# Projections, expert keys and the first output product on column tiles of 32, and the last exponents' turn exchanged with the first projection

## The chip, the cores and the metric

One core of one Trainium2 chip runs the whole kernel. The metric is device time in microseconds (us) of one execution; the kernel before takes 973.56 us, the median of 3 runs (973.54 to 974.25).

## The reference, cut to what matters

The input x has 128 batches, 64 features and 750 time steps. Everything is float32. In short:

```
h = token pooling of x            # windows of 8, softmax of a score over the window: [128, 94, 64]
n = layernorm(h)
q, k = n @ Q_h, n @ K_h           # 8 heads of rank 32, folded into one matrix per head: scores = n (K_h^T Q_h) n^T / 8
h = h + sum_h softmax(scores_h) @ n @ VO_h
n = layernorm(h)
sx = n @ hl_w                     # 4 heads of 16
q (4 experts), k, v of sx; causal softmax per head and expert; gate over the experts
h = h + two small layers, layernorm and a gate over the heads of that mixture
```

## The kernel before

The 128 batches are worked in 32 quads of 4 batches. A quad's data has 4 x 96 = 384 token columns (94 used). The instructions of every engine are written out by hand in a fixed order. One pass of `quad` holds parts of several quads at once: the token pooling of quads g+1 to g+3, the attention of quad g, the mix and the output product of quad g-1, the expert keys of quad g-2, and the expert attention of quad g-3. All stages exist for g = 3 to 31, which is 29 passes; those before fill the pipeline and those after drain it. Engines are ordered by semaphores only.

TensorE's order around the change is as follows (names of functions, then lines):

- `turn_p3(1, 5)` and `turn_p3(3, 4)` (L784), each four transposes of 128x96 shifted scores of the experts; ScalarE then takes their exponents out of PSUM with `exp_p3`.
- waits, among them for `s_shifted2` (VectorE's last subtraction, L1452) and for `r1_hx` (ScalarE has read bank 7).
- `project(.., 0, 0, 1)` (L687): the attention's first projection, two matmuls with 64 rows (rows 0 to 63 and 64 to 127 of the array) and 128 columns of weights, moving 384 columns, to banks 0 and 1. It sets `at_pa`.
- `turn_p3(6, 7)`: the last four transposes of the experts' scores, 128x128, to bank 7.
- `front_pair(1, 2, 3)` (L733): two matmuls of the same 64x128 form, to banks 2 and 3. It sets `f_kb`.
- waits for `exp_p3(3, 4)` (bank 4 is free) and for the first `copy_k` of the quad (`at_q`, bank 1 is free).
- `front_last(4, 1)`: one 64x128 matmul on rows 0 to 63 (L733) and, on rows 64 to 127, four matmuls with 96 columns of weights that move 64 columns each (L744). It sets `f_kc`.
- `pool_x` (L639, 128x32), `front_pair(0, 3, 7)` (L733, sets `f_ka`), `project(.., 1, 1, 6)` (sets `at_pb`), `mix` (L705, 32x64), `score` 0 (L695, 64x32 on 8 tiles, 376 columns).
- later `score` 1, `give_outT` (L713: eight matmuls with 128 rows and 64 columns, 192 moving columns), in every second quad `tok_score` (L625, L632), then `score` 2.

`turn_c` (L813, 128x32) multiplies, for each expert, four column tiles of mixed values with one moving operand of 84 columns.

ScalarE's order in the same stretch: `exp_p3(1)`, `exp_p3(3)`, `copy_k(1)` (waits for `at_pa`, reads bank 1, sets `at_q`), `exp_p3(6)`, two `front_kp` (wait for `f_kb`), `front_vc` (waits for `f_kc`, reads bank 1), one `front_kp`, `copy_k(0)`, `store_h`, `front_sxT` (waits for `f_ka`), `front_kp`, two `copy_k` (wait for `at_pb`).

In the trace each float32 matmul stands as two MATMUL records, each with its own LDWEIGHTS record. Below, one such record is called a pass. "64x128" means 64 rows and 128 columns of weights.

Of the kernel before, what the change touches and what calls it, by code (L numbers as in the profile page):

```python
# [15 lines left out]
TP = 96  # L16
HEADS, RANK = 8, 32
NH, NE, HD = 4, 4, 16
QB = 32
# [11 lines left out]
def exists(m, total):  # L31

    return not isinstance(m, int) or 0 <= m < total
# [10 lines left out]
def audio_tower(nc, x, tok_w, tok_b, attn_q, attn_k, attn_vo, hl_w, hl_b, wq, wk, wv, gate_w, gate_b,  # L44
                ln_g, ln_b, fc1_w, fc1_b, fc2_w, fc2_b, fnorm_g, fnorm_b, fgate_w, out):
    with ExitStack() as ctx:
        def sb(name, shape, dt=F32):
            return ctx.enter_context(nc.sbuf_tensor(name, shape, dt))

        def sem(name):  # L50
            return ctx.enter_context(nc.semaphore(name))


        psum = ctx.enter_context(nc.psum_tensor("psum", [128, 8, 512], F32))
# [9 lines left out]
        g_w = sb("g_w", [128, 2, 128])  # L64
        vo_w = sb("vo_w", [128, HEADS // 2, NFEAT])
# [68 lines left out]
        xT = sb("xT", [128, 2, 4, TP])  # L134
# [6 lines left out]
        cT = sb("cT", [128, HP, NT, 4, TB])  # L141
        oT = sb("oT", [128, NT, 2, TB])
        aq = sb("aq", [128, NE, NH, 32])
        wsx = sb("wsx", [128, NH, 32])
        wtok = sb("wtok", [128, 2, NH, HD])
# [24 lines left out]
        x3T = sb("x3T", [128, 4, TP])  # L170
# [89 lines left out]
        f_ka = sem("f_ka")  # L260
        f_kb = sem("f_kb")
# [9 lines left out]
        p_turned = sem("p_turned")  # L271
# [336 lines left out]
        def _(pe):  # L608
# [73 lines left out]
                mm.then_inc(at_turned, 1)  # L682

            def project(p, i, low, high):
                for half in range(2):
                    rows = slice(64 * half, 64 * half + 64)
                    mm = pe.matmul(psum[:, (low, high)[half], 0:4 * TP], g_w[rows, i, :], xT[rows, p, :, :].rearrange("p b t -> p (b t)"),  # L687
                                   start=True, stop=True)
                mm.then_inc(at_pa if i == 0 else at_pb, 1)

            def score(p, j, low, high):
# [17 lines left out]
            def give_outT(bank):  # L709

                for hp in range(HP):
                    for half in range(2):
                        mm = pe.matmul(psum[64 * half:64 * half + 64, bank, 0:NT * 64].rearrange("p (j c) -> p j c", j=NT), vo_w[:, hp, :],  # L713
                                       cT[:, hp, :, 2 * half:2 * half + 2, :].rearrange("p j b t -> p j (b t)"),
                                       start=(hp == 0), stop=(hp == HP - 1))
                mm.then_inc(at_outT, 1)

            def give_out(bank):
# [9 lines left out]
                    mm = pe.transpose(psum[:, bank, 128 * j:128 * j + 128], xn3[:, j, :, :].rearrange("p a f -> p (a f)"), ident)  # L728
                mm.then_inc(f_turned, 1)

            def front_k(half, w, bank):
                rows = slice(64 * half, 64 * half + 64)
                return pe.matmul(psum[:, bank, 0:NJ * 128], w[rows], x3T[rows, :, :].rearrange("p b t -> p (b t)"), start=True, stop=True)  # L733

            def front_pair(k, low, high):

                front_k(0, wsx[:, :, :].rearrange("p n d -> p (n d)") if k == 0 else aq[:, 1, :, :].rearrange("p n d -> p (n d)"), low)
                front_k(1, aq[:, 0 if k == 0 else 2, :, :].rearrange("p n d -> p (n d)"), high).then_inc(f_ka if k == 0 else f_kb, 1)

            def front_last(low, high):  # L740

                front_k(0, aq[:, 3, :, :].rearrange("p n d -> p (n d)"), low)
                for b in range(4):
                    mm = pe.matmul(psum[0:TP, high, 64 * b:64 * b + 64], x3T[64:128, b, :],  # L744
                                   wtok[64:128, 0, :, :].rearrange("k n d -> k (n d)"), start=True, stop=True)
                mm.then_inc(f_kc, 1)

            def front_resid(bank):
# [25 lines left out]
            def turn_p3(f, bank):  # L774
                j = ORDER[PT_J[f]]
                for e in range(NE):
                    if j == 2:
                        src, rows = pu3[2][:, e, f, :], TP
                    elif j == 1:
                        n, a = 2 * (f - 4) + e // 2, e % 2  # L780
                        src, rows = pu3[1][:, n, 2 * a:2 * a + 2, :].rearrange("p e u -> p (e u)"), 128
                    else:
                        src, rows = pu3[0][:, e, :, :].rearrange("p n u -> p (n u)"), 128
                    mm = pe.transpose(psum[0:rows, bank, 128 * e:128 * e + 128], src, ident)  # L784
                mm.then_inc(p_turned, 1)
# [43 lines left out]
            def quad(q):  # L829
                for v in range(4):  # L830
                    g = 4 * q + v
# [61 lines left out]
                            pe.wait_ge(x_scaled, 3 * g + 5)  # L893
                    if exists(g - 2, NQUAD):
                        pe.wait_ge(f_xT, g - 1)
                    if exists(g, NQUAD):
                        project(v % 2, 0, 0, 1)
                    if exists(g - 3, NQUAD):
                        turn_p3(6, 7)
                    if g + 1 == 0:  # L900
                        pe.wait_ge(tok_ready, ((g + 1) // 2) + 1)
                        make_g(0)
                    if exists(g - 2, NQUAD):
                        front_pair(1, 2, 3)
                        if exists(g - 3, NQUAD):
                            pe.wait_ge(p_copied, 7 * g - 17)
                        else:
                            pe.wait_ge(at_xT, g + 1)
                        if exists(g, NQUAD):
                            pe.wait_ge(at_q, 4 * g + 1)  # L910
                        else:
                            pe.wait_ge(s_shifted2, 2 * g - 4)
                    if exists(g + 1, NQUAD):
                        pe.wait_ge(x_scaled, 3 * g + 6)
                    if exists(g - 2, NQUAD):
                        front_last(4, 1)
# [9 lines left out]
                    if exists(g - 2, NQUAD):  # L926
                        front_pair(0, 3, 7)
                    if exists(g, NQUAD):
                        project(v % 2, 1, 1, 6)
# [158 lines left out]
            for q in range(-1, 12):  # L1088
                quad(q)

        @block.scalar
        def _(act):
# [34 lines left out]
            def copy_k(p, hp, bank):  # L1127
                act.activation(kp[:, p, :, hp, :], psum[:, bank, 0:4 * TP].rearrange("p (b t) -> p b t", b=4),  # L1128
                               ACT.Copy).then_inc(at_q, 1)
# [43 lines left out]
            def exp_p3(f, bank):  # L1173

                i = PT_J[f]
                j = ORDER[i]
                rows = TP if j == 2 else 128
                act.activation(pT3[j][:, f - (0, 4, 6)[i], :, :, :].rearrange("p e b t -> p (e b t)"), psum[0:rows, bank, :], ACT.Exp).then_inc(  # L1178
                    p_copied, 1)
# [21 lines left out]
            def quad(q):  # L1201
                for v in range(4):
                    g = 4 * q + v
# [55 lines left out]
                    if exists(g - 2, NQUAD):  # L1259
                        act.wait_ge(p_turned, 7 * g - 11)  # L1260
                        exp_p3(1, 5)
                        act.wait_ge(p_turned, 7 * g - 10)
                        exp_p3(3, 4)
                    if exists(g + 1, NQUAD):
                        act.wait_ge(at_pa, g + 2)
                        copy_k((v + 1) % 2, 1, 1)
                    if exists(g - 2, NQUAD):
                        act.wait_ge(p_turned, 7 * g - 9)
                        exp_p3(6, 7)
                    if exists(g - 1, NQUAD):  # L1270
                        act.wait_ge(f_kb, g)
                        front_kp((v + 1) % 2, 2, 3)
# [51 lines left out]
            for q in range(-1, 12):  # L1324
                quad(q)
# [398 lines left out]
```

## Time and profile before

| | |
|---|---|
| median of 3 runs | 973.56 us |
| the profiled execution's own time | 976.96 us |
| its span | 975.2 us |
| PE busy | 896.4 us (92%) |
| DVE, ACT, POOL busy | 815.2, 730.6, 718.2 us |

PE is TensorE's matmuls, PEld its weight loads, DVE is VectorE, ACT ScalarE, POOL GpSimd. Busy time of PE holds the modelled end of each matmul, so neighbouring groups overlap by some tenths of a microsecond; the starts are recorded. A row of windows gives the stretch, its length, the busy time (instructions) of PE, PEld, DVE, ACT and POOL, the granted TensorE clock (1.00 is 2.4 GHz), the DMA share and GB/s. Lines are those of the kernel before.

### The profile page before, as it was taken

The numbers are of one execution on the slowest core, as the hardware profiler recorded it, in microseconds if no ns is written. First come the engines' busy times: TensorE is split into PE (matmuls) and PEld (weight loads), VectorE is DVE, ScalarE is ACT, GpSimd is POOL, SyncE is SP. The second block draws the span as 40 slices with busy tenths as digits, with TensorE's granted clock in tenths as the row PEclk, the third lists the DMA queues.
The fourth block names the chain that finished last, engine by engine and source line by source line (L and its number), as shares of the span: only waits on it lengthen the run. The fifth ranks groups of instructions, "written<-read, shape, count | busy, mean of one in ns | idle before, by whom it ended". The sixth has DMA issues, their size and how long they took to land.

```text
span 975.2 us, 44187 instructions
## 1 busy us (share of the span) xinstructions
PE 896.4 (92%) x18600; PEld 572.2 (59%) x18600; DVE 815.2 (84%) x1917; ACT 730.6 (75%) x2759; POOL 718.2 (74%) x1052
## 2 busy tenths in 40 slices
PE   4788999999999999999999999999999999989841
PEld 4355656666666666666666666666666666556530
DVE  4455887889898988889898988989898998889877
ACT  1676788888878888888878888888778888885520
POOL 3233345677888887878888887878889888879893
PEclk9787999999999999999999999999999999999975
DMA  6310111110111101111111111111100000000001
GB/s 202 105 40 8 36 42 43 41 42 11 46 46 46 42 12 43 46 46 46 46 46 46 27 30 39 44 47 46 46 15 14 7 14 13 14 13 16 18 8 17
DMA packets 41157, 36.77 MB, mean 38 GB/s; under 512 B 27520, under 2 KB 30720, under 8 KB 40960
## 3 DMA queue, kind: packets, MB, share of 16 engines
q1 hardware_dynamic: 40406, 33.91, 12.4%
q8 instruction: 147, 2.41, 1.0%
q14 instruction: 50, 0.41, 0.1%
q10 hardware_dynamic: 554, 0.05, 0.0%
HBM read 25.08 MB, written 3.08 MB: 29 GB/s over the span
## 4 chain that ended last, share of the span: by engine, by line
PE 71%; ACT 16%; DVE 9%; POOL 2%; issue 1%; DMA 1%; POOLq 0%; ACTq 0%; DVEq 0%
ACT pu L1135 14%; PE psum L784 10%; PE psum L705 7%; PE psum L733 6%; PE psum L813 6%; PE psum L687 5%; PE psum L695 5%; PE psum L769 4%; PE psum L614 4%; PE psum L639 3%; PE psum L713 3%; PE psum L803 2%; PE psum L826 2%; PE psum L799 2%; DVE pu L1452 2%; PE psum L822 2%
## 5 line engine op out<-in xcount | busy, mean ns | idle before, releaser
L1135 ACT ACTIVATE pu<-psum,mx 128x94 f32<-128x94 f32 x768 | 247.4, 370 | 8.3 <-DVE mx L1420 6.9
L1135 ACT ACTIVATION_READ_ACCUMULATOR pu<-psum,mx 128x1 f32 x768 | 182.2, 238 | 0.0
L1420 DVE TENSOR_REDUCE mx<-psum 128x8 f32<-128x752 f32 x96 | 90.1, 940 | 88.0 <-PE psum L695 83.9
L478 POOL TENSOR_TENSOR pu<-pu,pr 128x752 f32<-128x752 f32 x96 | 138.7, 1447 | 28.0 <-DVE pr L1424 27.7
L1178 ACT ACTIVATE pT<-psum 96x512 f32<-96x512 f32 (+1 forms) x224 | 131.3, 601 | 36.3 <-PE psum L784 32.8
L512 POOL TENSOR_TENSOR st<-st,neg_half 128x12 f32<-128x12 f32 x64 | 146.0, 2281 | 5.0
L784 PE MATMUL psum<-ident_w,pu 128*96 128x128 f32 (+1 forms) x896 | 136.4, 283 | 13.1 <-ACT pu L1135 7.3
L1449 DVE TENSOR_REDUCE mx<-psum 128x16 f32<-128x1536 f32 (+2 forms) x96 | 116.4, 1213 | 10.3 <-PE psum L769 10.1
L784 PEld LDWEIGHTS psum<-ident_w,pu 128*96 128x96 f32 (+1 forms) x896 | 97.0, 134 | 47.4 <-issue 17.2
L1452 DVE TENSOR_TENSOR pu<-psum,mx 128x1536 f32<-128x1536 f32 (+2 forms) x96 | 117.6, 1225 | 3.3
L695 PE MATMUL psum<-kp,xT 64*32 64x376 f32 x1536 | 83.4, 491 | 8.3 <-ACT pu L1135 6.2
L1428 DVE STREAM_TRANSPOSE pT<-pu 128x768 f32<-128x768 f32 x96 | 87.7, 941 | 0.0
L733 PE MATMUL psum<-x3T,aq 64*128 64x384 f32 x256 | 79.6, 528 | 0.0
L1140 ACT ACTIVATE cT<-psum 128x384 f32<-128x384 f32 x128 | 53.9, 494 | 33.6 <-PE psum L705 33.5
L813 PE MATMUL psum<-gx,ct 128*32 128x84 f32 x3072 | 77.8, 240 | 0.9 <-issue 0.9
L813 PEld LDWEIGHTS psum<-gx,ct 128*32 128x32 f32 x3072 | 58.3, 110 | 25.5 <-issue 24.8
L1182 ACT ACTIVATE oc<-psum 128x336 f32<-128x336 f32 x96 | 43.1, 448 | 39.7 <-PE psum L813 39.5
L705 PE MATMUL psum<-pT,xn 32*64 32x384 f32 x1536 | 70.1, 489 | 0.3 <-ACT kp L1163 0.3
L1128 ACT ACTIVATE kp<-psum 128x384 f32<-128x384 f32 x128 | 59.9, 501 | 13.3 <-PE psum L687 13.3
L769 PE MATMUL psum<-kp,sxT 32*32 32x256 f32 (+2 forms) x3072 | 69.3, 390 | 0.0
L1460 DVE SCALAR_TENSOR_TENSOR ct<-sxT,psum 128x512 f32<-128x512 f32 x96 | 65.5, 682 | 3.7 <-PE psum L803 1.5
L529 POOL TENSOR_TENSOR ft<-ft,fx 128x192 f32<-128x192 f32 x29 | 17.2, 593 | 69.2 <-DVE ft L1528 69.2
(179 smaller groups left out, 2189.1 us busy)
## 6 DMA issues: line engine op xcount, KB each, us to landing
xs<-in_x SPq DMA_DIRECT2D x64, 375.0 KB, 3.9
vb<-va SPq DMA_DIRECT2D x32, 128.0 KB, 2.2
out_h<-ho SPq DMA_DIRECT2D x126, 16.0 KB, 1.4
out_h<-ho SPq DMA_DIRECT2D x126, 7.5 KB, 1.4
vc<-va SPq DMA_DIRECT2D x96, 16.0 KB, 2.3
gx<-in_L_ffn_gate_w SPq DMA_DIRECT2D x16, 0.2 KB
fc<-in_L_ffn_fc_w SPq DMA_DIRECT2D x12, 1.0 KB
fc<-in_L_ffn_fc_b SPq DMA_DIRECT2D x12, 0.1 KB
```

The lines of the kernel that those rows point to most:

```text
L478: pool.tensor_tensor(p, p, bcast(pr[:, j, :, :].rearrange("p a b -> p (a b)"), 2, NTOK), ALU.mult).then_inc(at_normed, 1)
L512: pool.tensor_tensor(st[:, k, 3, :], st[:, k, 2, :], neg_half[:, 0:NJ * NH], ALU.pow).then_inc(rstd, 1)
L695: mm = pe.matmul(psum[TB * b:TB * b + TB, (low, high)[par], 0:HP * NTOK], xT[rows, p, b, TB * j:TB * j + TB], kp[rows, p, b, :, 0:NTOK], s ...
L705: mm = pe.matmul(psum[64 * par:64 * par + 64, banks[b], 0:HP * TP], xn[rows, r, ub, 0, :], pT[rows, :, par, :, ub, :], start=(ub == 0), st ...
L733: return pe.matmul(psum[:, bank, 0:NJ * 128], w[rows], x3T[rows, :, :].rearrange("p b t -> p (b t)"), start=True, stop=True)
L769: mm = pe.matmul(psum[QB * b:QB * b + QB, bank + n, 0:NE * w].rearrange("p (e u) -> p e u", e=NE), sxT[rows, p, j, QB * b:QB * b + QB], kp ...
L784: mm = pe.transpose(psum[0:rows, bank, 128 * e:128 * e + 128], src, ident)
L813: mm = pe.matmul(psum[rows, bank, GC * e:GC * e + GC], mixed[:, rows], gx[:, e, :], start=True, stop=True)
L1135: ins = act.activation(pu[:, j, par, hp, 0:NTOK], psum[:, (low, high)[par], NTOK * hp:NTOK * hp + NTOK], ACT.Exp, bias=mx[:, j, par, hp:hp ...
L1178: act.activation(pT3[j][:, f - (0, 4, 6)[i], :, :, :].rearrange("p e b t -> p (e b t)"), psum[0:rows, bank, :], ACT.Exp).then_inc(p_copied, 1)
L1449: dve.tensor_reduce(mx3[:, i, :, :], S3(j, bank), AX.X, ALU.max).then_inc(shifted, 1)
L1452: dve.tensor_tensor(p, S3(j, bank), bcast(mx3[:, i, :, :], 3, QB * (j + 1)), ALU.subtract).then_inc(shifted, 1)
```

## The change

`project`, `front_pair` and `front_last` split their 64x128 matmuls into four of 64x32, each to its own 32 partitions of PSUM, and the 64x96 token matmuls into three of 64x32. `give_outT` splits each 128x64 matmul into two of 128x32. The moving columns of each matmul stay as they were. On TensorE `turn_p3(6, 7)` is moved ahead of the first projection, and on ScalarE `exp_p3(6, 7)` ahead of `copy_k(1)`.

```
             def project(p, i, low, high):
-                for half in range(2):
-                    rows = slice(64 * half, 64 * half + 64)
-                    mm = pe.matmul(psum[:, (low, high)[half], 0:4 * TP], g_w[rows, i, :], xT[rows, p, :, :]...
+                for c in range(4):
+                    for half in range(2):
+                        rows = slice(64 * half, 64 * half + 64)
+                        mm = pe.matmul(psum[32 * c:32 * c + 32, (low, high)[half], 0:4 * TP], g_w[rows, i, 32 * c:32 * c + 32], ...
...
             give_outT:
-                        mm = pe.matmul(psum[64 * half:64 * half + 64, bank, ...], vo_w[:, hp, :], cT[...], ...
+                        for c in range(2):
+                            q = 64 * half + 32 * c
+                            mm = pe.matmul(psum[q:q + 32, bank, ...], vo_w[:, hp, 32 * c:32 * c + 32], cT[...], ...
...
             def front_pair(k, low, high):
-                front_k(0, wsx[...] if k == 0 else aq[:, 1, ...], low)
-                front_k(1, aq[:, 0 if k == 0 else 2, ...], high).then_inc(f_ka if k == 0 else f_kb, 1)
+                for n in range(NH):
+                    front_k(0, n, wsx[:, :, :] if k == 0 else aq[:, 1, :, :], low)
+                    mm = front_k(1, n, aq[:, 0 if k == 0 else 2, :, :], high)
+                mm.then_inc(f_ka if k == 0 else f_kb, 1)
 
             def front_last(low, high):
-                front_k(0, aq[:, 3, ...], low)
+                for n in range(NH):
+                    front_k(0, n, aq[:, 3, :, :], low)
                 for b in range(4):
-                    mm = pe.matmul(psum[0:TP, high, 64 * b:64 * b + 64], x3T[64:128, b, :], wtok[...])
+                    for j in range(NJ):
+                        mm = pe.matmul(psum[QB * j:QB * j + QB, high, 64 * b:64 * b + 64], x3T[64:128, b, QB * j:QB * j + QB], wtok[...])
...
             TensorE's order:
+                    if exists(g - 3, NQUAD):
+                        turn_p3(6, 7)
                     if exists(g, NQUAD):
                         project(v % 2, 0, 0, 1)
-                    if exists(g - 3, NQUAD):
-                        turn_p3(6, 7)
...
             ScalarE's order:
+                    if exists(g - 2, NQUAD):
+                        act.wait_ge(p_turned, 7 * g - 9)
+                        exp_p3(6, 7)
                     if exists(g + 1, NQUAD):
                         act.wait_ge(at_pa, g + 2)
                         copy_k((v + 1) % 2, 1, 1)
-                    if exists(g - 2, NQUAD):
-                        act.wait_ge(p_turned, 7 * g - 9)
-                        exp_p3(6, 7)
```

## Rows read from the trace of the kernel before

**Rows 1.** Page, part 1: busy time of each engine.

```profile
PE 896.4 (92%) x18600; PEld 572.2 (59%) x18600; DVE 815.2 (84%) x1917; ACT 730.6 (75%) x2759; POOL 718.2 (74%) x1052
```

**Rows 2.** Windows of two neighbouring quads, the second with `tok_score`.

```profile
500.76:527.80 27.04, 26.39 (x555) 16.69 (x554) 24.59 (x59) 22.56 (x87) 23.18 (x35) 1.00 0.14 41
527.80:555.60 27.80, 27.75 (x602) 17.86 (x602) 24.55 (x59) 22.76 (x87) 22.45 (x33) 1.00 0.14 41
```

**Rows 3.** Waits of TensorE in the same two quads: total, times, longest.

```profile
PE psum L784 <- ACT pu L1135: 0.4, 1, 0.4
PE psum L695 <- ACT pu L1135: 0.2, 1, 0.2
```

**Rows 4.** Timeline of TensorE, from `turn_p3(1)` to `score` 0: start, length, passes.

```profile
499.79 1.04 PE L784 MATMUL psum<-ident_w,pu 128*96 128x128 f32 x8
500.76 0.92 PE L687 MATMUL psum<-xT,g_w 64*128 64x384 f32 x4
501.61 0.66 PE L784 MATMUL psum<-ident_w,pu 128*128 128x128 f32 x4
502.19 1.23 PE L733 MATMUL psum<-x3T,aq 64*128 64x384 f32 x5
502.95 0.56 PE L744 MATMUL psum<-wtok,x3T 64*96 64x64 f32 x5
...
503.35 0.41 PE L744 MATMUL psum<-wtok,x3T 64*96 64x64 f32 x3
503.69 0.86 PE L639 MATMUL psum<-xt,pick 128*32 128x192 f32 x16
504.48 0.59 PE L733 MATMUL psum<-x3T,wsx 64*128 64x384 f32 x1
...
505.23 0.81 PE L687 MATMUL psum<-xT,g_w 64*128 64x384 f32 x4
505.97 2.19 PE L705 MATMUL psum<-pT,xn 32*64 32x384 f32 x48
508.09 0.86 PE L695 MATMUL psum<-kp,xT 64*32 64x376 f32 x16
508.88 0.69 PE L826 MATMUL psum<-fc,hxm 128*128 128x96 f32 x4
```

**Rows 5.** Single lines in this quad: ns min/median/max, first and last start.

```profile
L687 PE MATMUL psum<-xT,g_w x8: 482/482/587, 500.8 to 505.6; 64*128 64x384 f32 x8
L695 PE MATMUL psum<-kp,xT x48: 474/475/500, 508.1 to 513.6; 64*32 64x376 f32 x48
L713 PE MATMUL psum<-cT,vo_w x16: 326/326/377, 511.4 to 512.6; 128*64 128x192 f32 x16
```

**Rows 6.** Timeline of TensorE's weight loads in `score` 0.

```profile
508.09 0.18 PEld L695 LDWEIGHTS psum<-kp,xT 64*32 64x32 f32 x16 [0.60 <-issue]
```

**Rows 7.** Timeline of TensorE before the next quad: `turn_c`, then transposes in a row.

```profile
522.34 0.80 PE L813 MATMUL psum<-gx,ct 128*32 128x84 f32 x32
...
526.39 0.60 PE L614 MATMUL psum<-ident_w,xs 128*128 128x128 f32 x4
526.83 1.04 PE L784 MATMUL psum<-ident_w,pu 128*96 128x128 f32 x8
```

**Rows 8.** Timeline of ScalarE in the stretch of rows 4.

```profile
500.43 1.08 ACT L1178 ACTIVATE pT<-psum 96x512 f32<-96x512 f32 x2 [0.49 <-PE psum L784]
501.72 0.49 ACT L1128 ACTIVATE kp<-psum 128x384 f32<-128x384 f32 x1 [0.21 <-PE psum L687]
502.30 0.60 ACT L1178 ACTIVATE pT<-psum 128x512 f32<-128x512 f32 x1
503.16 0.87 ACT L1163 ACTIVATE kp<-psum 128x384 f32<-128x384 f32 x2 [0.26 <-PE psum L733]
```

**Rows 9.** Timeline of VectorE: its last subtraction before this stretch, and its wait after it.

```profile
499.86 0.69 DVE L1452 TENSOR_TENSOR pu<-psum,mx 128x512 f32<-128x512 f32 x1
...
509.06 0.94 DVE L1420 TENSOR_REDUCE mx<-psum 128x8 f32<-128x752 f32 x1 [1.55 <-PE psum L695]
```

More of the change, by code:

```diff
@@ L684, in project @@
             def project(p, i, low, high):
-                for half in range(2):
-                    rows = slice(64 * half, 64 * half + 64)
-                    mm = pe.matmul(psum[:, (low, high)[half], 0:4 * TP], g_w[rows, i, :], xT[rows, p, :, :].rearrange("p b t -> p (b t)"),
-                                   start=True, stop=True)
+                for c in range(4):
+                    for half in range(2):
+                        rows = slice(64 * half, 64 * half + 64)
+                        mm = pe.matmul(psum[32 * c:32 * c + 32, (low, high)[half], 0:4 * TP], g_w[rows, i, 32 * c:32 * c + 32],
+                                       xT[rows, p, :, :].rearrange("p b t -> p (b t)"), start=True, stop=True)
                 mm.then_inc(at_pa if i == 0 else at_pb, 1)
@@ L712, in give_outT @@
                     for half in range(2):
-                        mm = pe.matmul(psum[64 * half:64 * half + 64, bank, 0:NT * 64].rearrange("p (j c) -> p j c", j=NT), vo_w[:, hp, :],
-                                       cT[:, hp, :, 2 * half:2 * half + 2, :].rearrange("p j b t -> p j (b t)"),
-                                       start=(hp == 0), stop=(hp == HP - 1))
+                        for c in range(2):
+                            q = 64 * half + 32 * c
+                            mm = pe.matmul(psum[q:q + 32, bank, 0:NT * 64].rearrange("p (j c) -> p j c", j=NT), vo_w[:, hp, 32 * c:32 * c + 32],
+                                           cT[:, hp, :, 2 * half:2 * half + 2, :].rearrange("p j b t -> p j (b t)"),
+                                           start=(hp == 0), stop=(hp == HP - 1))
                 mm.then_inc(at_outT, 1)
@@ L729, in front_turn, with front_k @@
                 mm.then_inc(f_turned, 1)
-            def front_k(half, w, bank):
+            def front_k(half, n, w, bank):
                 rows = slice(64 * half, 64 * half + 64)
-                return pe.matmul(psum[:, bank, 0:NJ * 128], w[rows], x3T[rows, :, :].rearrange("p b t -> p (b t)"), start=True, stop=True)
+                return pe.matmul(psum[32 * n:32 * n + 32, bank, 0:NJ * 128], w[rows, n, :], x3T[rows, :, :].rearrange("p b t -> p (b t)"),
+                                 start=True, stop=True)
             def front_pair(k, low, high):
-                front_k(0, wsx[:, :, :].rearrange("p n d -> p (n d)") if k == 0 else aq[:, 1, :, :].rearrange("p n d -> p (n d)"), low)
-                front_k(1, aq[:, 0 if k == 0 else 2, :, :].rearrange("p n d -> p (n d)"), high).then_inc(f_ka if k == 0 else f_kb, 1)
+                for n in range(NH):
+                    front_k(0, n, wsx[:, :, :] if k == 0 else aq[:, 1, :, :], low)
+                    mm = front_k(1, n, aq[:, 0 if k == 0 else 2, :, :], high)
+                mm.then_inc(f_ka if k == 0 else f_kb, 1)
             def front_last(low, high):
-                front_k(0, aq[:, 3, :, :].rearrange("p n d -> p (n d)"), low)
+                for n in range(NH):
+                    front_k(0, n, aq[:, 3, :, :], low)
                 for b in range(4):
-                    mm = pe.matmul(psum[0:TP, high, 64 * b:64 * b + 64], x3T[64:128, b, :],
-                                   wtok[64:128, 0, :, :].rearrange("k n d -> k (n d)"), start=True, stop=True)
+                    for j in range(NJ):
+                        mm = pe.matmul(psum[QB * j:QB * j + QB, high, 64 * b:64 * b + 64], x3T[64:128, b, QB * j:QB * j + QB],
+                                       wtok[64:128, 0, :, :].rearrange("k n d -> k (n d)"), start=True, stop=True)
                 mm.then_inc(f_kc, 1)
```

## The prediction

> **What bounds the kernel now.** I read the page's busy times first: TensorE is busy 92% of the span with VectorE next at 84% [rows 1]. An average can't say who ends last, so I took the windows of single quads. The middle of the run is a pair of quads of 27.04 and 27.80 us. In both TensorE is busy nearly all the time, 26.39 and 27.75 us; VectorE has 24.6 us of work, ScalarE 22.7, GpSimd 23, and the granted clock is 1.00, 2.4 GHz [rows 2]. Then the waits: in the two quads TensorE waits 0.4 us before the last transposes and 0.2 us before `score` 2, both times for ScalarE's exponents of the attention [rows 3]. So the quad has two parts. From `score` 0 to the end of these exponents ScalarE decides in every second quad, and TensorE has slack. From there through the next `score` 0 TensorE decides alone. The moved and re-tiled work lies in the second part, but for `give_outT`. VectorE waits 1.55 us for `score` 0 [rows 9], so it isn't what holds that part back. What is taken off TensorE there should shorten the quad; what is taken off between `score` 0 and `score` 2 is worth something only in the quads with `tok_score`, where TensorE doesn't wait.
>
> **What a block of matmuls costs.** The starts in rows 4 split a block into three pieces. A pass of 384 columns streams for 0.32 us: `front_pair(0)` and `project` 1 have the same form and follow each other, and each is two such passes on both row halves at once. A change of form costs a drain: `project` 1 has no change before it and one after, and takes 505.97 - 505.23 = 0.74 us, so the drain is 0.10 less the 0.01 by which its second tile starts later, about 0.09 us. The first weight load after the drain isn't hidden: the first pass is 587 ns long where the later ones are 482, so a load of 128 columns adds 0.105 us; with 64 columns it is 377 - 326 = 0.05, with 32 columns 500 - 475 = 0.025 us [rows 5]. `project` 0, with a change on both sides, then is 0.105 + 0.64 + 0.01 + 0.09 = 0.85, and the row says 501.61 - 500.76 = 0.85. `score` on eight 64x32 tiles is 508.88 - 508.09 = 0.79 for 376 columns: 0.627 of streaming, 0.025 of load, 0.09 of drain, and 0.05 by which the eighth tile starts after the first (some 6.5 ns each) [rows 4]. All eight stream together. That four column tiles may also read the same moving columns is shown by L813, whose four tiles share one moving operand: its 32 passes of 84 columns are over in 0.80 us [rows 7], and one at a time they would take 32 x 0.07 = 2.2.
>
> **The change on TensorE, in the quad of rows 4.** I lay the new order out on that clock.
>
> - The eight passes of `turn_p3(1)` and `(3)` start at 499.79. They take 8 x 0.109 = 0.87 (four transposes with no change of form take 526.83 - 526.39 = 0.44 [rows 7]). `turn_p3(6)` is of their form, so it follows at 500.66 with neither drain nor exposed load, and takes 0.44 where it took 502.19 - 501.61 = 0.58. Its wait is for VectorE's subtraction, done at 499.86 + 0.69 = 500.55 [rows 9], 0.11 before, and that is enough for a release of about 0.05. If it were late it would cost what it is late.
> - Drain, 0.09: `project` 0 starts at 501.19, 0.43 later than now. Its first pass takes 0.32 + 0.025, its second starts at 501.54 (the eighth tile at 501.58).
> - `front_pair(1)` now has the form of the block before it and starts at 501.86, without drain or load; it needs 0.64 and would be over at 502.50.
> - `front_last` waits for bank 1, which `copy_k(1)` must have read. `project` 0 ends at 501.58 + 0.48 = 502.06 (now 500.76 + 0.92 = 501.68). ScalarE starts 0.04 after the end and takes 0.49 [rows 8]: 502.59. With a release of some 0.06 the matmuls start at 502.66. That is a new stall of 0.16 us in a place that has none now. ScalarE itself is in time: its two exponents start 0.48 apart from 500.43, so `exp_p3(6)`, turned by 501.26, goes from 501.39 to 501.99, in front of the copy.
> - `front_last` from 502.66: four 64x32 tiles on rows 0 to 63 take 0.345 + 0.32 + 0.02 of stagger, then 0.09 of drain: 0.78, against 503.69 - 502.95 = 0.74 now. The tokens beside it are three tiles of eight short passes. Now they follow each other at 0.08 us: the eighth ends at 503.76 and lasts at most 0.25, so it starts at 503.51, (503.51 - 502.95) / 7. With 32 columns to load instead of 96 I take at most that, and at least the 0.053 that 64 columns stream; eight of them end with the keys or before. So `pool_x` starts at 503.44, 0.25 before its 503.69.
> - `pool_x` is unchanged, 0.79: 504.23. `front_pair(0)` takes 0.665 there, where it took 0.75, and `project` 1 takes 0.64 + 0.05 + 0.09 = 0.78 against 0.74. `mix` starts at 505.67, now 505.97.
>
> The sum is 0.30 us a quad in front of `mix`. By its terms: up to `front_last` one drain is left of three (0.18), and of first loads of 0.105, 0.05 and 0.105 one of 0.025 (0.235), with rounding and stagger 0.45 (503.0 - 502.5); `front_pair(0)` gives 0.085; against that stand 0.16 of stall, 0.04 in `front_last` and 0.04 of stagger in `project` 1.
>
> **What waits behind it.** ScalarE's copies for `f_kb` start at 501.86 + 0.32 + 0.05 + 0.48 = 502.71 where they start at 503.16 now [rows 8], and the later ones follow TensorE's 0.25 to 0.3 earlier. VectorE's 1.55 us before `score` 0 becomes 1.25. From `score` 0 on everything is shifted as one. The two waits of rows 3 stay as they are, since exponents and matmuls between them start from the same `score` 0. No DMA is moved, and no queue but those of TensorE and ScalarE.
>
> **`give_outT`.** Each tile still streams eight passes of 192 columns. The first load is 0.05 less 0.025, the stagger of two more tiles takes 0.013 back: 0.01 us. In the quads without `tok_score` it goes into the wait before `score` 2.
>
> **More instructions.** 86 more passes and as many loads a quad, to 555 or 602 now [rows 2]. In `score` 0 sixteen loads, with eight passes among them, are issued in 0.18 us [rows 6], 0.011 a load. A set of eight new passes needs 0.09 us of issue under 0.32 of streaming, so I cost it at nothing. If none of it were hidden it would be 86 x 0.011 = 0.95 us a quad, but `score` itself would then be longer than its row.
>
> One rule of the Trainium skill speaks against all this ("TensorE: Matmul & The Clock Gate", The mechanism): a weight load overlaps with running matmuls only if its row group differs. The column tiles of one block share their row groups, so by that rule each of the ten steps from one set of passes to the next would show its load, and the time would be that of the third rival. The trace says no: the sixteen loads of `score` 0 are all issued by 508.27, while its first passes run until 508.59, in the same row groups [rows 5, 6].
>
> **The sum.** 29 quads (g = 3 to 31) times 0.30 us is 8.7 us; `give_outT` adds 0.01 x 15 = 0.15, and the filling and draining quads, which have the projections or the keys but not both, about 0.3. Together 9.1 us. The profiled execution took 976.96 us by its own time (975.2 of span), 3.4 above the median; 9.1 less is 967.9 there and 964.5 against the median of 973.56.
>
> **Rivals.**
>
> - *No stall.* `front_last` doesn't have to wait, because `project`'s passes or the copy end earlier than modelled. Matmul ends are modelled in the trace, which speaks for it; that ScalarE now starts 0.04 after the modelled end speaks against. The gain is 0.46 x 29 = 13.4 us: 960.1. Chance 0.10.
> - *A wait takes half.* The pull of 0.3 us makes something else late: the subtraction before the moved transposes (0.11 in hand), or the bank of `front_last` (each 0.1 us more of ScalarE costs 0.1). At 0.15 a quad, 4.4 us remain: 969.2. For it: VectorE is busy 24.6 of 27.4 us [rows 2]. Against: it waits 1.55 once a quad. Chance 0.13.
> - *Loads show after all.* Ten steps x 0.025 us = 0.25 a quad, leaving 0.05: 1.5 us, 972.1. Against it rows 6, and `mix`, with six steps in 2.12 us where streaming is 1.92 [rows 4]. Chance 0.03.
> - *The tokens queue behind the keys.* In `front_last` the token passes are issued behind eight passes of keys instead of two. If they can't overtake the second set of keys, they start 0.36 late, and the block lasts 0.36 + 7 x 0.08 + 0.18 = 1.10 instead of 0.78 us. That takes the whole 0.30 and leaves 974.0. Against it: now the first token starts beside the key's first pass, 0.32 before its second [rows 4]. For it: only one waiting pass is overtaken there. Chance 0.04.
> - *Slower: the tokens go one at a time.* There are 24 token passes instead of 8, all on rows 64 to 127, short, and beside running keys. If their three column tiles don't overlap, they need 24 x 0.053 = 1.27 us, and with the 0.13 behind them `front_last` lasts 1.40 instead of 0.78. That costs 0.62, more than the 0.30: 0.32 x 29 = 9.3 us slower, 982.9. It decides from 0.04 us a pass on, where the block is 0.30 longer. Against it: L813, whose four tiles overlap at much the same size [rows 7]. For it: no block now mixes long and short passes on several column tiles. Chance 0.07.
>
> **How the numbers follow.** The forecast has 0.61. A measurement of this kernel can tell about 0.2%, 1.9 us, from no change. Faster: forecast, no stall and half, 0.84. Same: the two rivals that leave next to nothing, 0.07. Slower: the tokens one at a time, and 0.02 for something I don't see, 0.09. The range goes from 960.0, where the stall is gone, to 971.0, past the half gain, and leaves out the other cases.
>
> **What would show it.** After the change a quad pair should last 54.84 - 0.61 = 54.23 us; `turn_p3(6)` should follow at 0.109 a pass; `front_pair(1)` should start 0.67 after `project` 0; a wait of 0.16 for ScalarE's `kp` (L1128's copy) should stand before `front_last`; `mix` should start 5.88 after `turn_p3(1)`, now 6.18. I am wrong if the tile blocks last over 0.80 us, if the tokens reach past the keys, or if the waits for L1135 grow by what the front gave.

## The result: no faster, and 0.16% slower

The changed kernel takes 976.18 us (median of 22 runs, 973.21 to 978.31), the kernel before on the same chip 974.19 (22 runs, 973.12 to 975.73): ratio 1.0016, 95% interval 1.0009 to 1.0023. The forecast was 964.5. The profiled execution of after took 974.74 us (span 973.0); it lies 1.4 under its median, where that of before lay 2.8 above the 974.19. They differ in their first slices of granted clock, so their 2.2 us of difference are not a gain: I compare stretches at clock 1.00.

The page of after: busy times, part 2's clock in the run-in, the instruction queue of part 3, and the chain by engine.

```profile
PE 888.9 (91%) x21352; PEld 552.6 (57%) x21352; DVE 817.7 (84%) x1917; ACT 730.3 (75%) x2759; POOL 717.4 (74%) x1052
...
PEclk9897999999999999999999999999999999999975
...
q8 instruction: 169, 2.77, 1.2%
...
PE 72%; ACT 16%; DVE 7%; issue 2%; POOL 2%; DMA 1%; POOLq 0%; ACTq 0%; DVEq 0%
```

The same lines of before, whose busy times are in [rows 1]; the forecast did not use them:

```profile
PEclk9787999999999999999999999999999999999975
...
q8 instruction: 147, 2.41, 1.0%
...
PE 71%; ACT 16%; DVE 9%; POOL 2%; issue 1%; DMA 1%; POOLq 0%; ACTq 0%; DVEq 0%
```

2,752 more passes and as many loads, 22 more packets in the instruction queue, and "issue" is 2% of the chain where it was 1%. ("Issue" is time in which the engine waited for nothing that the profile shows. 42,704 TensorE instructions over 169 packets are 253 each, 37,200 over 147 also 253: a packet of 16 KB, 2.77 MB over 169, holds some 250 of them.)

The windows of after: the two neighbouring quads that answer to [rows 2], from `mix` to `mix`, then twenty quads at once.

```profile
505.28:532.23 26.95, 26.23 (x648) 16.11 (x640) 24.58 (x59) 22.56 (x88) 23.15 (x34) 1.00 0.15 43
532.23:559.93 27.70, 27.55 (x694) 17.41 (x686) 24.70 (x59) 22.78 (x88) 22.44 (x34) 1.00 0.14 40
...
202.61:752.02 549.41, 539.36 (x13258) 335.77 (x13251) 492.84 (x1154) 452.58 (x1721) 454.92 (x658) 1.00 0.14 39
```

The same twenty quads of before:

```profile
203.68:753.21 549.53, 541.99 (x11533) 345.72 (x11531) 490.86 (x1155) 452.98 (x1720) 455.27 (x658) 1.00 0.14 38
```

So there are two misses. An undisturbed pair of quads is 54.65 us where it was 54.84: 0.19 gained, not 0.61. And twenty quads don't keep even that: ten undisturbed pairs would be 546.5, and 549.41 passed, 2.9 more; before it was 548.4 and 549.53, 1.1 more.

TensorE's timeline in one quad of after, which answers to [rows 4]:

```profile
499.30 1.38 PE L790 MATMUL psum<-ident_w,pu 128*96 128x128 f32 x11
500.60 0.88 PE L688 MATMUL psum<-xT,g_w 64*32 64x384 f32 x16
501.27 1.43 PE L736 MATMUL psum<-x3T,aq 64*32 64x384 f32 x20
502.20 0.48 PE L750 MATMUL psum<-wtok,x3T 64*32 64x64 f32 x15
...
502.95 0.94 PE L639 MATMUL psum<-xt,pick 128*32 128x192 f32 x16
503.83 0.51 PE L736 MATMUL psum<-x3T,wsx 64*32 64x384 f32 x1
...
504.50 0.85 PE L688 MATMUL psum<-xT,g_w 64*32 64x384 f32 x16
505.28 2.19 PE L706 MATMUL psum<-pT,xn 32*64 32x384 f32 x48
507.40 0.86 PE L696 MATMUL psum<-kp,xT 64*32 64x376 f32 x16
```

ScalarE in the same stretch, as in [rows 8]:

```profile
499.82 1.57 ACT L1184 ACTIVATE pT<-psum 96x512 f32<-96x512 f32 x3 [0.49 <-PE psum L790]
501.58 0.49 ACT L1134 ACTIVATE kp<-psum 128x384 f32<-128x384 f32 x1 [0.19 <-PE psum L688]
502.23 0.87 ACT L1169 ACTIVATE kp<-psum 128x384 f32<-128x384 f32 x2 [0.15 <-PE psum L736]
```

Set from `project` 0 on, the forecast and these rows say: `front_pair(1)` at 0.67 and 0.67; first token of `front_last` at 1.5 and 1.60; `pool_x` at 2.25 and 2.35; `front_pair(0)` at 3.04 and 3.23; `project` 1 at 3.71 and 3.90; `mix` at 4.48 and 4.68. From the first transpose of `turn_p3(1)`, at 499.19, to `mix` it is 6.09 us; the forecast was 5.88, before it was 6.18. Every block on small tiles has the length that I gave it. What is missing stands in two places: 0.10 ahead of `front_last`, and 0.09 in `pool_x`, which now lasts 0.88 instead of 0.79 [rows 4]. The twelve transposes of `turn_p3` and `project` 0, at 500.60, are 1.41 apart: 12 x 0.109 and one drain.

What the quads lose on top is in other blocks. Two timelines of TensorE in after: `turn_c` where it is undisturbed, and one quad earlier where it isn't.

```profile
494.58 0.80 PE L819 MATMUL psum<-gx,ct 128*32 128x84 f32 x32
495.32 0.64 PE L790 MATMUL psum<-ident_w,pu 128*96 128x128 f32 x4
```

```profile
466.55 0.50 PE L819 MATMUL psum<-gx,ct 128*32 128x84 f32 x15
467.25 0.55 PE L819 MATMUL psum<-gx,ct 128*32 128x84 f32 x17 [0.20 <-issue]
467.73 0.64 PE L790 MATMUL psum<-ident_w,pu 128*96 128x128 f32 x4
```

From `turn_c` to `turn_p3` it is 0.74 us in the first and 1.18 in the second, in the middle of a block, and the profile shows nothing that the engine waited for. The DMA view of 464 to 469 us, in 40 slices of 0.125:

```profile
DMA  0000050000000000000000000000000000060000
...
q8 instruction: 2, 0.03, 2.9%
```

The only transfers are two packets of instructions, one begun at about 464.7, the next at 468.4. The late pass, at 467.25, comes 2.5 us after the first began. Between 91 and 860 us `turn_c` has 3 passes in before that stopped the block for over 0.1 us, 10 in after and 11 each in `e2` and `e4` (experiments below), and all 35 came 2.2 to 2.8 us behind the start of a packet; if they fell anywhere, some 13% of them would lie in that stretch (0.7 of 5.2 us, an estimate). In `mix` and `score` of `e2` it was 1.5 to 3.9.

In this trace two packets never begin less than 3.3 us apart, at the shortest 3.2 to 3.5 in the other kernels, though their mean distance is 5.2 here, 6.0 in before and 5.2 to 6.5 in the others. That isn't for want of demand. In an undisturbed stretch of after (a `mix3`, a `score3` and part of a `turn_c` lie in it) TensorE's 124 passes and 127 loads take 2.54 us:

```profile
519.46:522.00 2.54, 2.54 (x124) 1.80 (x127) 2.36 (x5) 1.86 (x5) 2.54 (x5) 1.00 0.04 10
```

Some 250 instructions per 3.3 us is 13 ns each, and in this stretch they go at 10. In a dense block sixteen loads and eight passes are issued in 0.18 us, 8 ns each [rows 6].

### The profile page after: what moved, and what is told of

Same layout as the page of the kernel before. It is cut to its first block, busy times and chain, and to the rows that moved or that the text cites. A ratio compares the mean times of both kernels' runs of the same rounds, so it can differ in the third digit from the quotient of the medians.

```text
span 973.0 us, 49691 instructions
## 1 busy us (share of the span) xinstructions
PE 888.9 (91%) x21352; PEld 552.6 (57%) x21352; DVE 817.7 (84%) x1917; ACT 730.3 (75%) x2759; POOL 717.4 (74%) x1052
## 3 DMA queue, kind: packets, MB, share of 16 engines
q8 instruction: 169, 2.77, 1.2%
## 4 chain that ended last, share of the span: by engine, by line
PE 72%; ACT 16%; DVE 7%; issue 2%; POOL 2%; DMA 1%; POOLq 0%; ACTq 0%; DVEq 0%
ACT pu L1141 14%; PE psum L790 10%; PE psum L706 7%; PE psum L819 7%; PE psum L736 6%; PE psum L696 5%; PE psum L688 5%; PE psum L775 5%; PE psum L614 4%; PE psum L639 3%; PE psum L716 3%; PE psum L809 2%; PE psum L832 2%; PE psum L805 2%; PE psum L828 2%
## 5 line engine op out<-in xcount | busy, mean ns | idle before, releaser
L1184 ACT ACTIVATE pT<-psum 96x512 f32<-96x512 f32 (+1 forms) x224 | 128.3, 600 | 33.8 <-PE psum L790 32.5
L790 PE MATMUL psum<-ident_w,pu 128*96 128x128 f32 (+1 forms) x896 | 129.9, 280 | 13.7 <-ACT pu L1141 7.2
L736 PE MATMUL psum<-x3T,aq 64*32 64x384 f32 x1024 | 82.3, 493 | 1.6
```

What stands on the lines that cost most here:

```text
L736: return pe.matmul(psum[32 * n:32 * n + 32, bank, 0:NJ * 128], w[rows, n, :], x3T[rows, :, :].rearrange("p b t -> p (b t)"), start=True, s ...
```

## The experiments

My theory after the result: the block model holds, the 0.10 is the wait for bank 1, and the rest is TensorE's supply of instructions. The rivals: the exchange or the tiles don't do what they say; the time is lost behind `score` 0. Each time below is a median, with the ratio to the kernel before on the same chip (its medians in the four rounds of experiments were 974.64, 974.42, 973.54 and 974.91). Kernels of different rounds are compared by their ratios. "Undisturbed pair" is the sum of the two lengths that neighbouring quads have when nothing is late, the second with `tok_score`, as in the windows above. Theories A to F are those of the texts on record.

**The exchange alone, on the old tiles** (`e1_order`; the new order of `turn_p3(6)`/`project` 0 and of `exp_p3(6)`/`copy_k(1)`, everything else as before).

> The kernel before with the exchange alone: turn_p3(6) ahead of project 0, exp_p3(6) ahead of copy_k(1), all matmuls on their old 64x128 tiles. Theory A (the added TensorE instructions cost what the tiles and the exchange gain; the exchange itself is sound): two drains of 0.09 and exposed loads of 0.05 and 0.105 us go, with rounding 0.37 us a quad, less a stall of 0.13 to 0.19 for copy_k, so 0.19 to 0.25 a quad: 967 to 968.5 us, ratio 0.993 to 0.9945, spread of the runs as before. Theory B (the new wait for bank 1 takes the gain, tiles cost nothing): the wait in front of front_last is as long as the gain, 973 to 975, ratio within 0.002 of 1.

972.5 us, ratio 0.9975 [0.9961, 0.9989]; undisturbed pair 54.62, 0.11 a quad less than before. That lies between the two theories: a part of the exchange's gain is left, and less than theory A gave. TensorE there:

```profile
501.25 0.92 PE L687 MATMUL psum<-xT,g_w 64*128 64x384 f32 x4
502.00 1.36 PE L733 MATMUL psum<-x3T,aq 64*128 64x384 f32 x5
502.81 0.63 PE L744 MATMUL psum<-wtok,x3T 64*96 64x64 f32 x5
...
503.63 0.86 PE L639 MATMUL psum<-xt,pick 128*32 128x192 f32 x16
504.42 0.59 PE L733 MATMUL psum<-x3T,wsx 64*128 64x384 f32 x1
```

The wait for bank 1 is here as well, and larger than forecast: `front_pair(1)` to `pool_x` takes 1.63 us, where 0.64 + 0.74 [rows 4] leave 0.25. `pool_x` has its old 0.79.

**The tiles alone, in the old order** (`e2_tiles`).

> The kernel after with the old order on TensorE and ScalarE: the column tiles alone. No wait for copy_k is expected in front of front_last. Theory A: blocks give 0.04 us a quad at most (first loads 0.05 + 0.08 + 0.085 less stagger 0.04 + 0.04 and 0.09 of pool_x starting apart), and the added instructions cost more: 975 to 979 us, ratio 1.001 to 1.005, runs spread over 3 us or more. Theory B: 0.13 a quad is gained, 970 us, ratio 0.996.

978.67 us, 1.0043 [1.0027, 1.0059]. One undisturbed pair, and the same twenty quads:

```profile
369.97:397.70 27.73, 27.58 (x694) 17.36 (x686) 24.72 (x58) 22.81 (x88) 22.44 (x34) 1.00 0.12 32
397.70:424.71 27.01, 26.32 (x648) 16.09 (x640) 24.59 (x59) 22.62 (x88) 23.20 (x34) 1.00 0.18 54
...
203.09:757.98 554.89, 544.87 (x13258) 336.46 (x13250) 492.86 (x1154) 453.71 (x1721) 455.63 (x658) 1.00 0.14 38
```

The pair is 0.10 shorter than before, and the twenty quads 5.4 us longer. Its late instructions aren't only in `turn_c`. The waits of TensorE from 91 to 860 us:

```profile
PE psum L819 <- issue: 2.8, 8, 0.6
...
PE psum L688 <- issue: 0.5, 2, 0.2
PE psum L706 <- issue: 0.3, 1, 0.3
```

And `mix`, which lasts 2.19 in every undisturbed quad, lasts this long in one of its worse ones:

```profile
702.47 2.97 PE L706 MATMUL psum<-pT,xn 32*64 32x384 f32 x46
```

**The wait for bank 1 taken away** (`e3_order_bank6` on the old tiles, `e4_after_bank6` on the new ones). `front_last`'s tokens go to bank 6, which is free by then, so the copy of bank 1 no longer stands in their way (TensorE waits for it only before `front_pair(0)`):

```diff
-                        if exists(g, NQUAD):
-                            pe.wait_ge(at_q, 4 * g + 1)
-                        else:
-                            pe.wait_ge(s_shifted2, 2 * g - 4)
...
-                        front_last(4, 1)
+                        front_last(4, 6)
...
-                        front_vc((v + 1) % 2, 1)
+                        front_vc((v + 1) % 2, 6)
```

> The exchange alone as in e1, and the tokens of front_last go to bank 6, which is free then, instead of bank 1, so front_last doesn't wait for copy_k(1). Both theories: the wait of e1 goes, 0.37 us a quad in all, 10.8 us: 962.5 to 964 us, ratio 0.989 to 0.990. If instead the copies of ScalarE were the bound there, no better than e1.

> The kernel after, with the tokens in bank 6. The wait of 0.27 us a quad in front of front_last goes. Theory A: 0.27 x 29 = 7.8 us less than after, 968 to 970, but 4 to 6 us more than e3, and a wider spread than e3. Theory B: as fast as e3 or faster, 961 to 964.

`e3`: 965.93 us, 0.9912 [0.9895, 0.9929]. `e4`: 967.02, 0.992 [0.99, 0.9939]. `e3` is 1.9 us above what both theories gave, and `e4` is not 4 to 6 us above `e3` but 1.1, with intervals that overlap. Twenty quads of `e3`, then of `e4`:

```profile
200.06:742.60 542.54, 535.23 (x11533) 347.88 (x11531) 491.16 (x1154) 451.50 (x1720) 455.32 (x658) 1.00 0.14 39
```

```profile
200.17:745.65 545.48, 534.69 (x13259) 338.44 (x13251) 492.41 (x1154) 450.76 (x1721) 455.05 (x658) 1.00 0.14 39
```

The exchange is worth 0.35 us a quad once nothing waits for the copy, 0.11 with the wait. With it the tiles have nothing left to give: undisturbed pairs 54.14 and 54.11, since most of the forms that they would make alike were brought together by the exchange, and the late instructions cost 4.4 us in `e4`'s twenty quads against 1.1 in `e3`'s.

**More instructions, nothing else** (`e5_split`, `e6_giveout`, `e12_split_score`). Three ways to add pairs of load and pass to the kernel before. `e5`: 80 a quad, each pass of `score` and of `score3`'s wide part cut into two halves of its columns, one right after the other on the same tile. `e6`: the change of `give_outT` alone, 16. `e12`: 48, `score` cut again, but with the halves outermost, so that neighbours are on different tiles:

```diff
-                for b in range(4):
-                    for par in range(2):
+                for k in range(2):
+                    for b in range(4):
+                        for par in range(2):
...
```

> The kernel before with 80 more load-and-pass pairs of TensorE a quad that bring nothing: score's matmuls of 376 moving columns are each two of 188, and score3's of 384 (j = 2) two of 192, on the same tiles, same order, same work. Theory A (each added instruction can cost, because TensorE's instructions aren't always there in time): slower than before by as much as the tiles alone, 976 to 980 us, ratio 1.002 to 1.006, with more quads longer than the usual 27.04 and 27.80 and more idle time put down to issue. Theory C (the loss of the tiles comes from the tiles themselves: their form, banks or row groups): as before, 974 to 975.5, ratio within 0.0015 of 1.

> The kernel before with give_outT alone on column tiles of 32: 16 more pairs a quad, in a place where a gain of 0.01 us is all there is. Theory A: 0 to 1.5 us slower. Theory C: 0.2 us faster, ratio within 0.001 of 1.

> The kernel before with 48 more pairs a quad that bring nothing, and without e5's fault: score sends the first halves (188 columns) of all eight tiles, then the second halves, so that no tile's passes stand in front of another tile's. Theory A: the block lasts 0.79 us as before, the undisturbed quads stay at 27.04 and 27.80, and late instructions add 1.5 to 4 us: 976 to 978.5. Theory C: as before, 974 to 975, or 0.1 a quad if the issue itself takes longer.

`e5`: 1001.65 us, 1.0287 [1.0273, 1.0301], outside both forecasts and no answer to the question, since its blocks themselves are longer (`score` 0.89 us instead of 0.79). `e6`: 976.83, 1.0027 [1.0015, 1.0039], at unchanged undisturbed quads: the gain of 0.01 that I gave `give_outT` isn't to be seen, and of the 2.4 us some stand in waits for "issue" in `turn_c`, 0.9 us in two places before and here, in 91 to 860 us:

```profile
PE psum L815 <- issue: 1.8, 5, 0.4
```

`e12`: 974.64, 1.0013 [1.0003, 1.0023], undisturbed quads unchanged. By the time alone that is what theory C gave; against before on the same chip the 48 pairs cost 1.1 us, barely clear of noise. A pair in `give_outT` cost more (2.4 us by 16 against 1.1 by 48; the two totals have overlapping intervals). So more instructions can cost time, and how much a pair costs depends on where it stands.

**Fewer instructions** (`e7_e3_turnc`, `e8_after_turnc`, `e9_e4_turnc`, `e13_before_turnc`). `turn_c`, the block in which most late passes show, can do with fewer: two of its three parts need a quarter of their passes when they are taken as whole tiles:

```diff
+                    if i < 2:
+                        mm = pe.matmul(psum[:, bank, GC * e:GC * e + GC], mixed, gx[:, e, :], start=True, stop=True)
+                        continue
                     for b in range(4):
                         rows = slice(QB * b, QB * b + QB)
...
```

> e3 (exchange, tokens in bank 6, old tiles), and turn_c(0) and (1) as matmuls of 128x128 instead of four of 128x32: 48 pairs a quad fewer. By the block model each then takes 8 x 0.109 = 0.87 us between transposes of its own form, where it takes 0.72 with 0.09 of drain ahead and 0.06 of load behind: no change of the undisturbed quad. Theory A: fewer pairs, fewer late instructions: 963.5 to 965, below e3's 965.9. Theory C: 965 to 967.

> The kernel after, with turn_c(0) and (1) as in e7: 38 pairs a quad more than before instead of 86. Theory A: the undisturbed quad stays at 26.95 and 27.70 and the long ones get fewer: 972.5 to 975, at least 1 us below after. Theory C: 975 to 977, as after.

> e4 (the kernel after with the tokens in bank 6) with turn_c(0) and (1) as 128x128 matmuls: 38 pairs a quad more than before instead of 86. Theory A (late instructions): the undisturbed quads stay at 26.68 and 27.44, the long ones go, 963.8 to 965.5, 1.5 us or more below e4's 967.0. Theory C (the tiles' form itself): 966.5 to 968.

> The kernel before with turn_c(0) and (1) as 128x128 matmuls: 48 pairs a quad fewer. Theory A (late instructions, more of them the denser the stream): the undisturbed quads stay 27.04 and 27.80, and the gain is what few late instructions there are, 0.5 to 1.5 us: 972.5 to 973.5. Theory E (turn_c in this form is simply shorter by 0.1 us a quad, whatever the tiles): 3 us or more, as on the kernel after, 970 to 971.

| based on | its ratio | with 48 pairs fewer | undisturbed pair |
|---|---|---|---|
| `e3` | 0.9912 | 965.22 (`e7`), 0.9909 [0.9896, 0.9923] | 54.14, 54.12 |
| after | 1.0016 | 972.97 (`e8`), 0.9987 [0.9978, 0.9997] | 54.65, 54.64 |
| `e4` | 0.992 | 962.49 (`e9`), 0.9895 [0.9874, 0.9917] | 54.11, 54.10 |
| before | 1 | 975.63 (`e13`), 1.0011 [0.9999, 1.0023] | 54.84, 54.83 |

By the ratios the two kernels on small tiles win 2.8 and 2.4 us (the intervals of `e4` and `e9` overlap, those of after and `e8` don't) though their undisturbed quads don't change; those on the old tiles win 0.3 and nothing. `e7` gained nothing that can be told from `e3`, as theory C had it. For `e13` both theories had given a gain, which did not come. It also rules out that the larger `turn_c` is faster by itself. `e9`'s twenty quads, 3.1 less than `e4`'s:

```profile
198.82:741.19 542.37, 533.90 (x12298) 349.50 (x12290) 491.71 (x1154) 451.05 (x1721) 454.89 (x658) 1.00 0.14 39
```

**Small tiles only where neighbours have them** (`e11_e7_late_tiles`): `e7` with `front_pair(0)` and `project` 1 alone on 64x32, between `pool_x` and `mix`, 24 pairs a quad fewer than the kernel before.

> e7 (exchange, tokens in bank 6, old tiles, turn_c(0) and (1) 128x128) with only front_pair(0) and project 1 on 64x32 tiles: 24 pairs fewer a quad than before. By the block model one first load of 0.105 becomes 0.025 and 0.04 of stagger is added: 0.04 us a quad, 26.64 and 27.40, 963.5 to 964.5 against e7's 965.2. Theory A allows that, since the count stays below that of before. Theory C: 965 to 966.

963.82 us, 0.9901 [0.9885, 0.9917], with the least spread of all (962.79 to 964.33). Undisturbed pair 54.02; in the twenty quads hardly anything is late, ten pairs being 540.2:

```profile
199.46:739.82 540.36, 533.26 (x11058) 354.79 (x11050) 490.13 (x1155) 450.82 (x1721) 454.63 (x658) 1.00 0.14 39
```

**The tokens at their old 96 columns** (`e10_e4_tokens96`: `e4`, and in `front_last` 8 token passes of 64x96 beside key passes of 64x32).

> e4 with the four token matmuls on their old 64x96 form, beside keys on 64x32: 16 pairs a quad fewer. Theory A: pool_x, whose four tiles start 0.109 us apart in the kernel after instead of 0.02, because its instructions come late behind 24 short token passes, starts together again: 0.09 us a quad less, 26.60 and 27.35, 964 to 965.5. Theory D (a change of the number of columns inside a block costs a drain): front_last gets 0.1 to 0.3 us longer, 967 to 974.

988.81 us, 1.0158 [1.0139, 1.0178], above both forecasts. One quad of it:

```profile
509.38 1.49 PE L736 MATMUL psum<-x3T,aq 64*32 64x384 f32 x24
510.80 0.89 PE L749 MATMUL psum<-wtok,x3T 64*96 64x64 f32 x8
511.62 0.86 PE L639 MATMUL psum<-xt,pick 128*32 128x192 f32 x16
```

The tokens no longer run beside the keys. They start after the last key pass, 1.42 us after `front_pair(1)` did, and the quad is 0.74 longer. The Trainium skill ("TensorEngine Tiling (Array Packing)", Key Properties) says that a change of the tiling mode drains TensorE; the trace agrees in so far as nothing overlaps here: the only change from `e4` is that the tokens have 96 columns beside keys of 32, so that pair of forms is such a change, inside a block too. Not every change of the column count is one: before, keys of 128 columns and tokens of 96 did overlap [rows 4].

**The tokens' order** (`e14_tokens_between`: `e9` with three token passes, then a key pass, four times, so that `pool_x` stands behind a long pass).

> e9 with front_last's matmuls issued in another order: three token tiles, one key tile, four times over, so that the block ends on a long key pass. Theory A: pool_x's instructions have time to come, its tiles start within 0.02 us of each other, and a quad is 0.05 to 0.09 us shorter: 26.60 and 27.35, 960 to 961.5. Theory F (pool_x waits tile by tile for the column tiles of front_last to become free): no change, or longer since the last key starts later: 962 to 965.

971.92 us, 0.9966 [0.9954, 0.9978], slower than either theory gave. Starts of `pool_x` and `front_pair(0)`:

```profile
528.41 0.86 PE L639 MATMUL psum<-xt,pick 128*32 128x192 f32 x16
...
529.20 0.51 PE L736 MATMUL psum<-x3T,wsx 64*32 64x384 f32 x1
```

`pool_x` is back at 0.79 (0.86 in `e9`), so its extra time in after comes from what stands right before it. But the last key pass now starts late, `front_last` is 0.27 longer (from `front_pair(1)` to `pool_x` 1.69 us, in `e9` 1.42), and the kernel loses 7 us to `e9` by the ratios.

**`give_outT` on its old tiles in the best kernel** (`e15_e9_old_give_outT`, 16 pairs fewer).

> e9 with give_outT on its old 128x64 tiles, 16 pairs a quad fewer. Theory A: 0.0 to 2 us less than e9's 962.5. Block model alone: 0.01 us longer in every second quad, 962.6.

966.61 us, 0.9913 [0.9901, 0.9926]: no gain against `e9`'s 0.9895 (966.61 lies above the forecast of 962.6; the intervals just overlap, and which is faster stays unclear), though 16 pairs a quad are gone and the undisturbed quads are `e9`'s. Its twenty quads, 1.9 longer than `e9`'s:

```profile
202.39:746.61 544.22, 535.32 (x11978) 350.95 (x11970) 491.74 (x1155) 451.61 (x1721) 455.39 (x658) 1.00 0.14 39
```

## Why the prediction was wrong

- **"More instructions ... so I cost it at nothing."** This is the step that failed. The issue of a new set does hide under the streaming of the last, as I had it. But it isn't issue that was short, it is the supply: the instructions arrive in packets of some 250, at the shortest 3.3 us apart, and the stretch of `mix3`, `score3` and `turn_c` needs them faster, 250 in 2.54. With 86 more pairs a quad a packet is asked for every 5.2 us instead of 6.0, and more dense blocks find theirs on the way. What it costs: 7.6 us in twenty quads of `e2`, 4.4 in `e4`, 2.9 in the profiled execution of after, against 1.1 before. I had looked for the cost where the instructions are added; it falls on blocks that the change doesn't touch. The row was on the page of before all the time (`q8`), and so was 0.9 us of waits for "issue" in `turn_c`.
- **The stall, 0.16.** It was 0.26: the first tokens start 1.60 after `project` 0, and with the keys 0.03 earlier that is 1.57, not 1.31 as the streaming alone would have it. Two short steps were too small in the forecast: ScalarE starts 0.10 after the modelled end of `project` 0 (500.60 + 0.88, then 501.58), where I took 0.04 from the old form, and TensorE 0.10 after the copy, not 0.06. `e3` and `e4` show what the stall is worth: without it the exchange brings 0.35 a quad. The rival *no stall* gave 0.46; `e4` has 0.37, and `pool_x`'s 0.09 is the difference.
- **`pool_x` unchanged, 0.79.** It was 0.88 in after, 0.86 in `e9`, and 0.79 in `e1` (old tiles) and `e14` (a long pass before it). With the 24 short token passes right before it, its four tiles start up to 0.11 apart, in `e1` and `e14` within 0.02. With only 8 token passes before it (`e10`) it is 0.79 too. It fits that short passes use up the head start that issue has over streaming, but no run shows that by itself. I had asked whether the tokens would be in time, and not who comes behind them.
- **Sum.** 0.30 less 0.10 less 0.09 is 0.11, and a quad gained 0.09 to 0.10. Times 29 that is 2.8 us. The medians say 2.0 slower, so 4.8 us stand against it. The profiled executions show 1.8 us more of late instructions in twenty quads of after than of before, which would be 2.6 in 29 (an estimate); the other 2.2 are not accounted for. With `pool_x`, the added instructions that I had cost at nothing took 2.6 + 2.6 = 5.2 us, the stall's error 2.9.
- **What held.** Drains, first loads, four column tiles at once, the moved transposes at 0.109 a pass, tokens beside the keys (`front_last` 0.78), and no growth in the waits of [rows 3] (0.4 and 0.3 us in this pair of quads). The rule that loads overlap only with another row group ("TensorE: Matmul & The Clock Gate" of the Trainium skill, The mechanism) doesn't hold here either: in after all sixteen loads of `front_pair(0)` are over by 504.01, its first eight passes run until 504.34, and the second eight, on the same row groups, start at 504.17 and last 0.48 us where the first last 0.51, so that their loads don't show. Of the rivals, the tokens queueing or going one at a time didn't happen, and *a wait takes half* had the mechanism of the 0.10, a quarter of the 11.7 us between forecast and result. None had the instruction supply. By the forecast's own measure of 0.2% the ratio of 1.0016 is "same", which had 0.07, but from two rivals that didn't happen; what did happen had no more than the 0.02 "for something I don't see".

One page bears on this cause. "Runtime: NRT & Kernel Launch" of the Trainium skill, Instruction fetch mechanics, says that instructions come in blocks of 16 KiB, 256 of them, and that this is hidden because the sequencer dispatches more slowly than the memory fills. The trace agrees on the size (16 KB packets, 253 instructions each) and not on the hiding: dense blocks issue at 8 ns an instruction, and packets bring at most one in 13.

**What stays open.** That late instructions cost time which the undisturbed quads don't show is shown: by the late passes and their distance to a packet, by `e6` and, barely, `e12` (more pairs, same undisturbed quads, slower), and by `e8` against after and, with overlapping intervals, `e9` against `e4` (fewer pairs, same undisturbed quads, faster). How much a given kernel loses isn't a matter of the count: `e13` gained nothing with 48 pairs fewer, and neither did `e15` with 16 fewer. It fits that what decides is where in a quad the ends of the packets fall, but I made no experiment that moves these ends alone. The 2.2 us that are missing in the sum are open too. Part of them may go with the granted clock of the run-in: of after's 22 executions the seven with a mean granted clock of 0.970 or more, the profiled one (0.971) among them, have a median of 974.74 us, the other fifteen 976.77. In the four rounds of experiments 35 of 73 executions of before were at 0.970 or more, and their median was 0.3 to 1.4 us below that of the rest of their round. These counts are too few to say whether after gets the lower clock more often.

**The best version** is `e9` (0.9895), or `e11` (0.9901), which is steadier; they can't be told apart. Both beat the kernel before by some 10 us and after by 11 to 12. Most of it is the exchange with bank 6 (`e3`, 8.6 us).

## What to carry to other kernels

- Passes and loads aren't free because they hide under streaming: look at the instruction queue and at waits for "issue", and count pairs in the densest stretch, wherever the new ones stand.
- When a step moves, ask which bank its neighbour writes and who still reads it. Here the new order brought 0.11 us a quad with the old bank and 0.35 with a free one.
- Compare undisturbed stretches and long ones: the first shows whether the block model is right, the second what is lost at random.

## What the runs showed that I had not expected

- Split passes cost when both halves of a tile are issued right after each other. In `e5` the 64 half passes of `score3`'s wide block take twice the time of the 32 passes that they replace; first `e5`, then before:

```profile
529.43 1.90 PE L772 MATMUL psum<-kp,sxT 32*32 32x192 f32 x64
```

```profile
544.30 0.93 PE L769 MATMUL psum<-kp,sxT 32*32 32x384 f32 x32
```

  With neighbours on different tiles (`e12`) the same doubling in `score` leaves the quad as it was, while in `e5` each `score` is 0.1 longer. What holds the other tiles up in `e5` isn't shown.
- Key passes of 128 columns and token passes of 96 overlap; key passes of 32 and token passes of 96 don't (`e10`, 0.74 us a quad).
